# Graph layer with linear attention and a routed feed-forward stage: the one-hot buffer holds a whole block in two halves, and VectorE's list makes each batch half a block further on

## The reference

```
xn = layernorm(x)
agg[v] = mean over the edges (s -> v) of xn[s]
g = relu(agg @ W_l.T + b_l + xn @ W_r.T) + xn
q, k = elu(xn @ wq + bq) + 1, elu(xn @ wk + bk) + 1        # 8 heads of 32
v = xn @ wv + bv
kv, k_sum = sum over nodes of k v^T (each head), sum over nodes of k
m = (q kv) / (q . k_sum + 1e-6) @ wo + bo
x = x + g + m
y = layernorm(x)
logits = mean over nodes of y @ Wr + br ; two softmaxes with a capacity rule give the two chosen experts and their gates
x = x + layernorm(sum of the two gated experts gelu(y @ W1[e] + b1[e]) @ W2[e] + b2[e], added to y) * gamma + beta
```

## Time and profile before

| | us |
|---|---|
| median of 3 runs | 2843.47 |
| lowest, highest | 2842.36, 2846.12 |
| the profiled execution's own time | 2852.55 |
| its span | 2851.1 |
| GpSimd busy with the 1661 gathers | 1594.4 |
| first and last gather begin at | 137.6, 2236.7 |
| TensorE, VectorE busy in the span | 2072.7, 1423.2 |

### The profile page before, as it was taken

The page is one execution under the profiler, slowest core; times in us unless marked ns, Lnnn a source line. Parts: engine busy times, 40 slices in busy tenths (PEclk is TensorE's granted clock), DMA queues, the critical chain, the costliest instruction groups (busy, mean ns, idle before and its releaser), DMA issues.

```text
span 2851.1 us, 35328 instructions
## 1 busy us (share of the span) xinstructions
PE 2072.7 (73%) x10858; PEld 1578.6 (55%) x10858; DVE 1423.2 (50%) x3244; ACT 954.7 (33%) x2221; POOL 1603.2 (56%) x1679
## 2 busy tenths in 40 slices
PE   0077777789889876666666666666666599999998
PEld 0055555556656644444444444444444389999997
DVE  8823233345665644344344344344344367777777
ACT  5633233223333321221221221221221255555655
POOL 1077777777777777777777777777777200000000
PEclk9999989989998887888777887888777699999999
DMA  8744444344444444444444444444444222222222
GB/s 238 225 133 133 133 133 128 104 123 143 138 145 138 139 126 123 122 124 123 123 123 123 122 123 123 123 123 123 123 122 123 67 77 77 78 66 66 66 66 69
DMA packets 205191, 340.31 MB, mean 119 GB/s; under 512 B 33118, under 2 KB 151131, under 8 KB 205115
## 3 DMA queue, kind: packets, MB, share of 16 engines
q0 software_dynamic: 80160, 219.14, 27.0%
q1 hardware_dynamic: 124538, 119.81, 13.3%
q10 hardware_dynamic: 416, 0.39, 0.1%
HBM read 288.01 MB, written 51.20 MB: 119 GB/s over the span
## 4 chain that ended last, share of the span: by engine, by line
POOL 47%; PE 27%; issue 16%; DVE 4%; DMA 3%; ACT 1%; POOLq 1%; SPq 1%; ACTq 0%; DVEq 0%
POOL ring L672 47%; PE pd L1295 10%; PE pa L1280 5%; PE pc L1280 5%; PE pd L1095 2%; DMA ring<-xn_table,idxb 2%; PE pd L1106 1%; DVE bst L1343 1%; PE pa L1248 1%; PE pa L1249 1%; PE pd L1088 1%; PE pd L996 1%; DMA yT<-in_x 1%; PE pd L1109 0%; DVE ring L1409 0%
## 5 line engine op out<-in xcount | busy, mean ns | idle before, releaser
L672 POOL DMA_INDIRECT ring<-xn_table,idxb x1661 | 1594.4, 960 | 633.3 <-issue 491.0
L1248 PE MATMUL pa<-ring,ohh 128*128 128x256 f16 x1661 | 486.4, 308 | 566.4 <-DMA ring<-xn_table,idxb 511.5
L1248 PEld LDWEIGHTS pa<-ring,ohh 128*128 128x128 f16 x1661 | 180.6, 109 | 693.6 <-issue 500.7
L1249 PE MATMUL pa<-ring,ohh 128*128 128x257 f16 x1661 | 491.5, 312 | 0.0
L1295 PE MATMUL pd<-parts 128*128 128x256 f32 (+1 forms) x1568 | 312.2, 283 | 1.8 <-DVE parts L1750 1.8
L1295 PEld LDWEIGHTS pd<-parts 128*128 128x128 f32 (+1 forms) x1568 | 253.4, 188 | 10.3 <-DVE parts L1750 2.4
L768 ACT ACTIVATE ring<-pa 128x257 f32<-128x257 f32 x196 | 75.4, 385 | 533.8 <-PE pa L1249 533.8
L1511 DVE TENSOR_TENSOR ohh<-pc,edges 128x512 f16<-128x512 f32 (+1 forms) x307 | 211.6, 717 | 67.3 <-PE pa L1249 61.7
L1095 PE MATMUL pd<-mats,work 128*128 128x256 f32 x784 | 233.1, 424 | 11.7 <-ACT work L851 10.8
L1249 PEld LDWEIGHTS pa<-ring,ohh 128*128 128x128 f16 x1661 | 180.9, 109 | 105.1 <-issue 32.4
L1295 PE MATMUL pd<-W_lo_t,parts 128*128 128x256 f32 x784 | 219.9, 281 | 0.0
(11 more groups left out here) (205 smaller groups left out, 3482.5 us busy)
## 6 DMA issues: line engine op xcount, KB each, us to landing
ring<-xn_table,idxb POOLq DMA_INDIRECT x1661, 2.8
yT<-in_x SPq DMA_DIRECT2D x48, 512.0 KB, 4.4
xn_table<-ring SPq DMA_DIRECT2D x24, 512.0 KB, 5.4
x_rows<-work SPq DMA_DIRECT2D x48, 256.0 KB
y_rows<-work SPq DMA_DIRECT2D x48, 256.0 KB
work<-y_rows SPq DMA_DIRECT2D x24, 512.0 KB, 4.3
work<-x_rows SPq DMA_DIRECT2D x24, 512.0 KB, 3.8
out<-work SPq DMA_DIRECT2D x24, 512.0 KB, 3.1
```

The source lines that it names most:

```text
L672: pool.indirect_dma_start(out=msgs[:, k, 0:PARTS * D], out_offset=None, in_=xn_table[:, :], in_offset=bass.IndirectOffsetOnAxis(ap=idxb[:, ...
L1248: mm(pa[:, t % 2, 0:D], oh[:, slot, :], msgs[:, k, 0:D], start=begins, stop=False, skip_group_check=True)
L1249: ins = mm(pa[:, t % 2, 0:D + 1], oh[:, slot, :], msgs[:, k, D:2 * D + 1], start=False, stop=ends, skip_group_check=True)
```

## The change

The number of places for one-hots goes from 17 to 34. Half of them stay in `ohh`; the other half lie at the end of `ring`. Batches 0 to 3 of a block (tiles 0 to 16) are in the first half, batches 4 to 7 in the second. VectorE may now make batch n when TensorE is done with batch n - 8. Each place j of a list makes batch j + 4, counted on into the next block. Four batches are made ahead of the first block where there were two, so the shadow and double lists run four batches ahead where they ran two, and `stage3` four where it ran none. The batches that read the row of numbers from SBUF are 86 where they were 84. GpSimd's and ScalarE's lists are the same, TensorE's too but for the place it reads one-hots from.

```diff
-    SLOTS = TB // 2
+    SLOTS = TB
+    LEAD = NBT // 2
...
-        ohh = sb("ohh", [P, SLOTS * WIN], F16)
+        ohh = sb("ohh", [P, SLOTS // 2 * WIN], F16)
...
+        OH2 = XR1 + 2 * D
+        assert OH2 + SLOTS // 2 * WIN // 2 <= RING
+        oh_halves = [v.rearrange("p (k w) -> p k w", w=WIN)
+                     for v in (ohh[:, :], ring[:, OH2:OH2 + SLOTS // 2 * WIN // 2].bitcast(F16))]
...
-            def one_hots(b, q):
+            def one_hots(b, j):
+                if isinstance(b, int):
+                    b, q = divmod(NBT * b + j + LEAD, NBT)
+                else:
+                    b, q = b + (j + LEAD) // NBT, (j + LEAD) % NBT
+                if is_int(b, NB) or not batch_tiles(b, q):
+                    return
                 ks = batch_tiles(b, q)
-                if not ks:
-                    return
-                wait(dve, s["batch_used"], NBT * b + q - NBT // 2 + 1)
-                m, slot = len(ks), ks[0] % SLOTS
+                wait(dve, s["batch_used"], NBT * b + q - NBT + 1)
+                m, half, slot = len(ks), ks[0] // (SLOTS // 2), ks[0] % (SLOTS // 2)
...
-                row = iota_f[:, :] if isinstance(b, int) and NBT * b + q < NBT * DELAY + 4 else pc[:, 0, :]
-                V.tensor_tensor(oh[:, slot:slot + m, :], bc(row[:, c0:c0 + WIN], m), where, ALU.is_equal)\
+                row = iota_f[:, :] if isinstance(b, int) and NBT * b + q < NBT * DELAY + 2 + LEAD else pc[:, 0, :]
+                V.tensor_tensor(oh_halves[half][:, slot:slot + m, :], bc(row[:, c0:c0 + WIN], m), where, ALU.is_equal)\
                     .then_inc(s["oh_ready"], 1)
...
             def shadow_block(b, u):
-                one_hots(b, 2)
-                one_hots(b, 3)
+                one_hots(b, 0)
+                one_hots(b, 1)
...
-                one_hots(b + 1, 0)
-                one_hots(b + 1, 1)
+                one_hots(b, 6)
+                one_hots(b, 7)
...
-            one_hots(0, 0)
-            one_hots(0, 1)
+            for j in range(-LEAD, 0):
+                one_hots(0, j)
```

More of the change, by code:

```diff
@@ L155, in build_layer @@
         assert MSGS + KEPT * SW <= RING
-        oh = ohh[:, :].rearrange("p (k w) -> p k w", w=WIN)
         at = {"yT": DELAY * C * BN, "ring": 0}
@@ L210, in build_layer @@
         xr = [xr0, ring[:, XR1:XR1 + 2 * D]]
-        assert XR1 + 2 * D <= RING
+        OH2 = XR1 + 2 * D
+        assert OH2 + SLOTS // 2 * WIN // 2 <= RING
+        oh_halves = [v.rearrange("p (k w) -> p k w", w=WIN)
+                     for v in (ohh[:, :], ring[:, OH2:OH2 + SLOTS // 2 * WIN // 2].bitcast(F16))]
         late_at = [0, PART_WORDS]
@@ L1239, in stage3 @@
                             pe.wait_ge(s[f"gathered{q}"], batch_gathers(b, q))
-                        slot = k % SLOTS
+                        slot = k % (SLOTS // 2)
                         t = LO[k] // STRIP
@@ L1247, in stage3 @@
                             pe.wait_ge(s["iota_placed"], 1)
-                        mm(pa[:, t % 2, 0:D], oh[:, slot, :], msgs[:, k, 0:D], start=begins, stop=False, skip_group_check=True)
-                        ins = mm(pa[:, t % 2, 0:D + 1], oh[:, slot, :], msgs[:, k, D:2 * D + 1], start=False, stop=ends,
+                        mm(pa[:, t % 2, 0:D], oh_halves[k // (SLOTS // 2)][:, slot, :], msgs[:, k, 0:D], start=begins, stop=False, skip_group_check=True)
+                        ins = mm(pa[:, t % 2, 0:D + 1], oh_halves[k // (SLOTS // 2)][:, slot, :], msgs[:, k, D:2 * D + 1], start=False, stop=ends,
                                  skip_group_check=True)
@@ L1603, in shadow_block @@
                     feature(first, pr)
-                one_hots(b, 4)
+                one_hots(b, 2)
                 if b > 0:
                     keep_sums(b - 1, pd[:, 3, :])
-                one_hots(b, 5)
+                one_hots(b, 3)
                 for pr in range(2):
                     add_bias(second, pr)
-                one_hots(b, 6)
+                one_hots(b, 4)
                 for pr in range(2):
                     feature(second, pr)
-                one_hots(b, 7)
+                one_hots(b, 5)
                 for kq in third:
@@ L1641, in double_block @@
                 query_features(d + 1)
-                if b + 1 < 2 * DELAY:
-                    one_hots(b + 1, 0)
-                    one_hots(b + 1, 1)
+                one_hots(b, 6)
+                one_hots(b, 7)
                 normalise_queries(d + 1)
-            one_hots(0, 0)
-            one_hots(0, 1)
+            for j in range(-LEAD, 0):
+                one_hots(0, j)
             for b in range(DELAY):
```

## The result

| | before | after |
|---|---|---|
| median of 20 runs each, us | 2844.74 | 2840.64 |
| lowest, highest | 2841.35, 2850.43 | 2839.03, 2843.61 |
| the profiled execution's own time | 2852.55 | 2840.60 |
| its span | 2851.1 | 2839.1 |

The ratio is 0.9985, with a 95% interval of 0.9978 to 0.9992: the change makes the kernel 4.1 us faster, which is clear of no change but less than the 0.2% that the forecast called telling. The forecast was 2841.0.

A forecast was written before the change was run, and what follows sets the result against it. GpSimd, issuing gathers without pause, was taken as the bound. Shadow blocks -3.2, double blocks -0.5 and 0 elsewhere summed to -3.7 us, shaded to -2.5 from the median 2843.47: 2841.0 us, 8-in-10 range 2836 to 2850.

The forecast's parts named there:

- GpSimd sets the pace: In the gathers' part, 137.6 to 2237.7 us, GpSimd never waits beyond its fixed step of 0.305 us between two gathers.
- VectorE's waits are worth nothing: VectorE's 112.2 us of waits for TensorE before one-hot batches nearly all go, to under 20, but gain no time.
- TensorE's waits would fall from 23.6 us to nothing: TensorE's weight loads and matmuls stop waiting for one-hots; hidden by the ring of gathers, so worth 0.0, at most 23.6 us.
- The shadow blocks, -3.2 us: Of 10.0 us gather excess, waited batches' 5.9 us goes, long rows add 2.3, two more batches 0.4; bounds -5.9 to +9.2.
- the five rows: Five profiled waited batches in the shadow blocks, costing gathers 0.22 us on average, taken for all 27: 5.9 us.
- The double blocks, -0.5 us: Of 7.5 us gather excess, line 1523 ending earlier gives -1.2 us; `join_strips` meeting a gather costs nothing, or up to +5.
- The tie: A gather beginning together with a VectorE instruction pays nothing; in double blocks `join_strips` would begin with the gather of 672.07.
- The loop, 0.0: The loop's 4.6 us of gather excess stays, since lines 1520, 1555 and 1565 keep their times; bounds -1 and +1.
- The shading to -2.5: The summed gain of -3.7 us was cut to -2.5 us because its weightiest step is an average of five rows.
- A: Rival: rows behind the features pay what the waited batches paid, or the mean stays 0.22; 2843.9 us, chance 0.17.
- B: Rival: in shadow and double blocks, VectorE instructions start just ahead of gathers; +7 us, 2850.5 us, slower; chance 0.14.
- C: Rival: TensorE's 23.6 us of waits on one-hots held back gathers; 2819.9 us, or 2831.7 with half; chance 0.05.

## Why the prediction was right, and where its steps were off

**GpSimd sets the pace: right.** No gap of GpSimd is longer than 0.3 us after the change, and the stretch of the gathers shortened by what their durations did, 5.0 us.

**VectorE's waits are worth nothing: right.** They went to zero, more fully than the 20 us that I allowed, and GpSimd's gaps are the same 505.6 us before and after, so none of the 112.2 us had reached it. The deep buffer with the old places, which has no such waits, left the time as it was (0.0 to 0.1% over before), but that was measured only where TensorE was late, and there it had waits of TensorE of its own.

**TensorE's waits would fall from 23.6 us to nothing: wrong.** The rows add up to 26.8 us. The step took them at their word, but in the profile after they name the wrong half of the buffer and are waits for gathers, and before only 4.5 of the 23.6 us were waits on one-hots. Those did go. It did not touch the sum, since the term was priced at 0.0.

**The shadow blocks, -3.2 us: too large.** They gave 10.2 - 8.4 = 1.8 us, summed by gathers. The mechanism is as told: before, batches from `iota_f` covered the start of 28 lengthened gathers for 7.3 us; after, 18 for 4.0 us. The two terms of that step can be read from the traces. Of the 27 waited batches one reads PSUM, and the other 26 had made gathers pay 4.5 us, not 5.9: the five rows stood for a mean of 0.22 where it was 0.17. And each long row of eight after the change pays once, 0.20 to 0.51 us, then 0.08 at most. But line 1526 then met gathers at four borders with 0.05 to 0.11 us in hand and cost 0.44 to 0.51 us each (with two smaller ones 2.5 us, where it had cost 1.2), a place for which I had no term in these blocks.

**The double blocks, -0.5 us: too small.** They gave 6.5 - 4.7 = 1.8 us. The tie came as reckoned at 667.75 and at four more borders; line 1526 costs 1.0 us over the ten blocks. I had taken it as free before, from one border, while it had cost 1.6 us. Line 1529 gave 0.4 us, not the 1.2 reckoned, since only five borders had the form of the earlier trace rows. Lines 1561 and 1571 gave 0.3 us, and one batch from `iota_f` another 0.3, for which I had no term. Errors of opposite sign in the stages left the sum at -3.7, against -5.0 measured: that it is so near is in part luck.

**The loop, 0.0:** 6.4 - 5.0 = 1.4 us, a little over the bound of 1. Line 1571 gave 0.9 of it; the step held that the moments of these lines would stay, and they did not.

**The shading to -2.5** was unneeded: the unshaded sum of -3.7 us lies nearer to 4.1. That the point came out at 2841.0 against 2840.64 owes 1.3 us to a median of before that 20 runs put higher than three, and is luck.

**The rivals.** A (the excess only changes hands) is refused by 23.1 to 18.1 us in the whole, though it describes line 1526. B (the long rows catch more gathers) is what happens at single borders, not in the sum. C (the waits were worth time) is refused where GpSimd sets the pace: only 4.5 of its 23.6 us were there to win, and no gap of GpSimd became shorter. Where TensorE is late the places of the batches do give 0.2 to 0.5%; by what way is not shown. The inference of the Trainium skill ("SBUF — State Buffer", section "Who interferes with whom") that tensor_tensor does not delay the making of descriptors is refused by the kernel that reads the row from SBUF: 18 to 20 us more of GpSimd's time.

**Not settled.** What made the engines stand still in the comparisons is unknown, so no experiment shows a time that follows GpSimd's busy time at an undisturbed pace. The evidence for that link is the pair of profiles of before and after and their 20 runs each. How much GpSimd's excess differs between two executions of one kernel at the undisturbed pace is not known either, since there is one profile of each; nor was the share of the deeper buffer and of the new places measured there.

## What to carry to other kernels

Before pricing a wait that a change removes, look at the idle times of the engine that sets the pace: if each is its fixed step, no wait elsewhere costs time, and what is left to win is in the durations of its own instructions. A long duration there is caused by what another engine was doing when it began, so look at the timeline of the two side by side, and try keeping an input in PSUM where that is free (here it took those meetings away, and its gain in time was not measured). A row that says who released a wait is to be checked against the buffer that was read.

## What was not expected of the hardware

A gather is delayed only by a VectorE instruction with two inputs in SBUF that began at least some 0.04 us before it. Over all meetings in the two profiles, with VectorE up to 0.03 us ahead the gather takes 0.95 us, and VectorE's instruction takes some hundredths more (0.73 for 0.68 at 667.75); from 0.05 us ahead the gather pays (in between, both were seen), and it pays the rest of the instruction less 0.13 us, 0.52 us at most for 0.69. Such a VectorE instruction of 128x512 that begins later than 0.04 us into a gather is not lengthened: 405 of them took 675 to 694 ns. After a delay the next gather begins 1.12 us after the end of the instruction that caused it. In a row at steps of 0.60 us the third instruction further on begins 1.11 us after that same end. The two begin within 0.01 us of each other, which is a tie, so a row of such instructions pays once and then meets the gathers nearly for nothing.
